# Two per-sample 64x64 channel mixes with residuals: the first loads reordered, the index column turned on TensorE

## The chip, the cores and the metric

One core of one Trainium2 chip runs the kernel. The metric is the device time of one execution in microseconds. The kernel before was timed three times: 92.57 us in the median, 92.44 to 92.94. All data is fp32, x and the output are 16.78 MB each.

## The reference

Both layers act on channels only, so one sample b needs one 64x64 matrix: with A = I + w0[subject[b]] and B = I + w1[condition[b]], the output is (A B) transposed, times x[b].

```python
def reference(x, itok_B_0_7, itok_B_1_198, L0_cond_weights, L1_cond_weights):
    # x (128, 64, 512); L0 weights (8, 64, 64); L1 weights (200, 64, 64)
    x = x + jnp.einsum('bct,bcd->bdt', x, L0_cond_weights[itok_B_0_7])
    x = x + jnp.einsum('bct,bcd->bdt', x, L1_cond_weights[itok_B_1_198])
    return x
```

## The kernel before

Everything of x fits in SBUF (`xy`, 128 KB of each partition) and is overwritten in place by the output, so loads never wait for a free buffer. The 128 samples are cut into 32 slots of four samples; two slots are a unit (8 samples, 1 MB of x), and there are 16 units.

**Start.** SyncE issues the condition indices `cond` (128 numbers, one to each partition, L129), then x of unit 0 (L130) and the first slot of unit 1 (L131). It then waits at L133 for `s_w0b_early`, which VectorE has finished raising when the 16 first-layer matrices of units 0 and 1 are picked, and issues the other slot of unit 1 and units 2 to 15 (L134 to L136). ScalarE issues the first-layer weights `w0_rows` (128 KB, L370) and the indices `subjects` (L372). GpSimd builds the identity matrix (L142, L144), waits for `cond` (L147) and issues the gather (L148): 128 rows of 16 KB of the second layer's weights, row b to partition b, 2.1 MB.

**First layer.** TensorE turns `w0_rows` (L171); VectorE adds the identity into `w0t` (L349) and copies the 16 picks of units 0 and 1 (L360). GpSimd copies the other 112 picks once the gather has landed (L163).

**Ticks.** From the landing of `w0_rows` ScalarE makes TICKS dummy copies (L378), and after each of them TensorE makes three dummy transposes (L176). They compute nothing that is used; TensorE meets its work behind them only when the last is done.

**Second layer.** When the gather has landed, VectorE adds 1 to the diagonals (L365), TensorE turns the matrices in 16 turns of four (L186), and VectorE and ScalarE copy them out of PSUM (L269) in turn. TensorE then multiplies the pairs of matrices (`products`, L206), VectorE and ScalarE write them to `m_diag` (L276, L295), and TensorE applies them to x (`apply_single` L247 for unit 0, `apply` L225 for the rest). Each result is copied over x by the two engines (L303, L282), and ScalarE issues one store for each finished unit (L312, L315), the last unit in two halves of 512 KB.

**Queues.** SyncE's DMAs are q1 in the profile, ScalarE's q10, GpSimd's gather q0. All of them run on the same 16 DMA engines.

Of the kernel before, what the change touches and what calls it, by code (L numbers as in the profile page):

```python
# [5 lines left out]
def bass_cond_residual_kernel(  # L6
# [24 lines left out]
    fp32 = mybir.dt.float32  # L31
    i32 = mybir.dt.int32
    ALU = mybir.AluOpType

    B, C, T = x_dram.shape
# [24 lines left out]
    EARLY = 2  # L60


    TICKS = 18
    WARM = 3
    POOL = mybir.EngineType.Pool
    DVE = mybir.EngineType.DVE
# [8 lines left out]
    with ctx:  # L75
        def sb(name, shape, dt):
            return ctx.enter_context(nc.sbuf_tensor(name, shape, dt))

        def sem(name):
            return ctx.enter_context(nc.semaphore(name))  # L80
# [7 lines left out]
        m_diag = sb("m_diag", [P, 2, M_RING, J, P], fp32)  # L88
        ident = sb("ident", [P, P], fp32)
        mask = sb("mask", [P, 2], fp32)  # L90
        cond = sb("cond", [B, 1], i32)
        subjects = sb("subjects", [1, B], i32)

        psum = ctx.enter_context(nc.psum_tensor("psum", [P, 8, BANK], fp32))
        w0_psum = psum[0:C, 7, :]

        s_cond = sem("s_cond")
        s_subjects = sem("s_subjects")
        s_w0_rows = sem("s_w0_rows")
# [19 lines left out]
        s_x = [sem(f"s_x{n}") for n in range(UNITS)]  # L119
# [4 lines left out]
        @block.sync  # L124
        def _(sp):
            def load(s, n):
                sp.dma_start(xy[:, s:s + n, :], x_view[:, s:s + n, :]).then_inc(s_x[s // 2], 16)

            sp.dma_start(cond[:, :], cond_dram.rearrange("(b o) -> b o", o=1)).then_inc(s_cond, 16)  # L129
            load(0, 2)  # L130
            load(2, 1)  # L131

            sp.wait_ge(s_w0b_early, EARLY * UNIT)  # L133
            load(3, 1)  # L134
            for v in range(2, UNITS):
                load(2 * v, 2)  # L136
            for v in range(UNITS):
                sp.wait_ge(s_out[v], 32 if v < SINGLE or v == UNITS - 1 else 16)

        @block.gpsimd  # L140
        def _(pool):
            nc.gpsimd.memset(ident[:, :], 0.0).then_inc(s_zeros, 1)  # L142
            pool.wait_ge(s_zeros, 1)
            nc.gpsimd.affine_select(out=ident[:, :], in_=ident[:, :], compare_op=ALU.not_equal, fill=1.0,  # L144
                                    base=0, pattern=[[-1, P]], channel_multiplier=1).then_inc(s_ident, 1)

            pool.wait_ge(s_cond, 16)  # L147
            nc.gpsimd.indirect_dma_start(  # L148
                out=w1_rows[:, :, :].rearrange("b d e -> b (d e)"), out_offset=None,
                in_=w1_dram.rearrange("s d e -> s (d e)"),  # L150
                in_offset=bass.IndirectOffsetOnAxis(ap=cond[:, 0:1], axis=0)).then_inc(s_gather, 16)

            pool.wait_ge(s_subjects, 16)
            for first in range(EARLY * UNIT, B, 2 * UNIT):
                _, picked = nc.values_load_multi_w_load_instructions(  # L155
                    subjects[0:1, first:first + 2 * UNIT], engines=(POOL,), min_val=0, max_val=S0 - 1,
                    skip_runtime_bounds_check_because="subjects index the 8 matrices")
                if first == EARLY * UNIT:
                    pool.wait_ge(s_gather, 16)
                    pool.wait_ge(s_w0t, 4)  # L160
                for n in range(2 * UNIT):
                    v, odd, r = (first + n) // UNIT, n // SLOT % 2, n % SLOT
                    nc.gpsimd.tensor_copy(w0b[HALVES[odd], v * SLOT + r, :],  # L163
                                          w0t[HALVES[odd], bass.ds(picked[n] * C, C)]).then_inc(s_w0b, 1)

        @block.tensor
        def _(pe):
            pe.wait_ge(s_ident, 1)
            pe.wait_ge(s_w0_rows, 16)
            for z in range(ROWS):  # L170
                last = nc.tensor.transpose(w0_psum[:, z * P:(z + 1) * P], w0_rows[:, z, :], ident[:, :])  # L171
# [39 lines left out]
            def apply(k):  # L211

                first, n = BLOCKS[k]
                pe.wait_ge(s_m_v, 2 * (k + 1))
                pe.wait_ge(s_m_s, 2 * (k + 1))
                for s in range(2 * first, 2 * (first + n)):
                    v, odd = s // 2, s % 2
                    pe.wait_ge(s_x[v], 32 if v == 1 else 16)
                    if s >= Y_RING:

                        pe.wait_ge(s_y_v, 2 * (s - Y_RING + 1))
                        pe.wait_ge(s_y_s, 2 * (s - Y_RING + 1))
                    for j in range(J):
                        for h, rows in enumerate(HALVES):
                            last = nc.tensor.matmul(psum[:, 2 * (s % Y_RING) + h, :],  # L225
                                                    m_diag[rows, odd, v % M_RING, j, :],
                                                    xy[rows, s, j * T:(j + 1) * T],
                                                    start=j == 0, stop=j == J - 1)
                    last.then_inc(s_y_psum, 1)

            def apply_single(k):

                v = BLOCKS[k][0]
                pe.wait_ge(s_m_v, 2 * (k + 1))
                pe.wait_ge(s_m_s, 2 * (k + 1))
                pe.wait_ge(s_x[v], 32 if v == 1 else 16)
                for half in range(2):
                    s = 2 * v + half
                    if s >= Y_RING:

                        pe.wait_ge(s_y_v, 2 * (s - Y_RING + 1))
                        pe.wait_ge(s_y_s, 2 * (s - Y_RING + 1))
                    for j in range(J):
                        for h in range(2):
                            rows = QUARTERS[2 * half + h]
                            for odd, columns in enumerate(HALVES):
                                last = nc.tensor.matmul(psum[columns, 2 * (s % Y_RING) + h, :],  # L247
                                                        m_diag[rows, odd, v, j, 0:C],
                                                        xy[rows, 2 * v + odd, j * T:(j + 1) * T],
                                                        start=j == 0, stop=j == J - 1)  # L250
                    last.then_inc(s_y_psum, 1)
# [83 lines left out]
        @block.vector  # L335
        def _(dve):
            for r, rows in enumerate(QUARTERS):
                for b in range(2):
                    nc.vector.memset(mask[rows, b:b + 1], 1.0 if b == r % 2 else 0.0).then_inc(s_mask, 1)

            dve.wait_ge(s_ident, 1)
            dve.wait_ge(s_subjects, 16)
            dve.wait_ge(s_w0_turned, 1)

            turned = w0_psum.rearrange("q (y j s k) -> q j s k y", y=J, j=J, s=S0)
            one = ident[0:C, 0:C].rearrange("q (o k y j) -> q j o k y", o=1, y=J, j=J)
            for rows in HALVES:
                for j in range(J):
                    nc.vector.tensor_tensor(  # L349
                        w0t[rows, :].rearrange("q (s j k y) -> q j s k y", s=S0, j=J, y=J)[:, j, :, :, :],  # L350
                        turned[:, j, :, :, :],
                        one[:, j, :, :, :].to_broadcast((C, S0, Q // J, J)), ALU.add).then_inc(s_w0t, 1)

            _, picked = nc.values_load_multi_w_load_instructions(
                subjects[0:1, 0:EARLY * UNIT], engines=(DVE,), min_val=0, max_val=S0 - 1,
                skip_runtime_bounds_check_because="subjects index the 8 matrices")
            dve.wait_ge(s_w0t, 4)
            for n in range(EARLY * UNIT):
                v, odd, r = n // UNIT, n // SLOT % 2, n % SLOT
                nc.vector.tensor_copy(w0b[HALVES[odd], v * SLOT + r, :],  # L360
                                      w0t[HALVES[odd], bass.ds(picked[n] * C, C)]).then_inc(s_w0b_early, 1)

            dve.wait_ge(s_gather, 16)
            diagonal = w1_rows[:, :, :].rearrange("b d e -> b (d e)")[:, ::C + 1]
            nc.vector.tensor_scalar_add(diagonal, diagonal, 1.0).then_inc(s_w1_plus, 1)  # L365
            copies(dve, nc.vector.tensor_copy, nc.vector.tensor_scalar_mul, s_w1_v, s_m_v, s_y_v, 0)

        @block.scalar
        def _(act):
            act.dma_start(w0_rows[:, :, :], w0_dram.rearrange("s (k j) d -> (s k) j d", j=ROWS)  # L370
                          ).then_inc(s_w0_rows, 16)
            act.dma_start(subjects[:, :], subject_dram.rearrange("(o b) -> o b", o=1)).then_inc(s_subjects, 16)  # L372

            act.wait_ge(s_w0_rows, 16)
            for n in range(TICKS):
                if n >= 1:
# [31 lines left out]
```

## Time and profile before

| | |
|---|---|
| median of three runs | 92.57 us |
| profiled execution | 92.7 us, of which the span is 90.8 us and 1.9 us lie around it |
| TensorE / VectorE / ScalarE / GpSimd busy | 85% / 66% / 63% / 26% of the span |
| moved by DMA | 35.93 MB, 396 GB/s over the span |
| mean granted TensorE clock | 0.968 |

Times inside the kernel count from the start of the span. "Share" of DMA is the busy share of the 16 DMA engines and can read slightly above 1. Bytes are booked in the slice in which a packet begins; a packet of the gather is 16 KB, one of x 4 KB, so short slices in the gather's time jump up and down.

### The profile page before, as it was taken

How to read it: one execution, taken by the hardware profiler on the slowest of the kernel's cores; microseconds unless marked ns; L12 is line 12 of the kernel's file. 1: busy time of each engine (PE TensorE's matmuls, PEld its weight loads, DVE VectorE, ACT ScalarE, POOL GpSimd, SP SyncE). 2: the span in 40 equal slices, each digit the busy share in tenths (PEclk: the TensorE clock that was granted, in tenths of full speed). 3: DMA queues.
4: the chain of work that ended last, by engine and by line, in shares of the span. 5: the costliest groups of instructions: out<-in, count | busy, mean ns of one | idle time of the engine just before them, and what ended most of it. 6: DMA issues, size and time to landing. Idle time of an engine off the chain costs nothing.

```text
span 90.8 us, 2458 instructions
## 1 busy us (share of the span) xinstructions
PE 76.8 (85%) x906; PEld 42.9 (47%) x906; DVE 60.0 (66%) x124; ACT 57.0 (63%) x114; POOL 23.5 (26%) x119
## 2 busy tenths in 40 slices
PE   0599959977999999999999999999999999992000
PEld 0489749965545443544544454454444444440000
DVE  1096019994388787978878788888787887887000
ACT  2899807885367675867776677777576775775000
POOL 3400049989998988000000000000000000000000
PEclk9999999999999999999999999999999999999755
DMA  0999999999999999999999999999999999999992
GB/s 6 337 446 424 455 361 415 420 399 409 409 413 402 409 418 394 419 418 424 411 415 426 415 413 420 420 422 420 411 415 422 420 419 428 404 424 420 419 399 103
DMA packets 9453, 35.93 MB, mean 396 GB/s; under 512 B 737, under 2 KB 866, under 8 KB 9314
## 3 DMA queue, kind: packets, MB, share of 16 engines
q1 hardware_dynamic: 4512, 16.78, 46.1%
q10 hardware_dynamic: 4786, 16.91, 45.8%
q0 software_dynamic: 144, 2.10, 5.4%
q8 instruction: 7, 0.11, 0.5%
q14 instruction: 4, 0.03, 0.1%
HBM read 19.01 MB, written 16.78 MB: 394 GB/s over the span
## 4 chain that ended last, share of the span: by engine, by line
PE 68%; DMA 12%; DVE 9%; issue 1%; DVEq 1%; ACTq 0%; POOLq 0%
PE psum L225 58%; DMA w_rows<-in_L_cond_weights_dram,cond 10%; DVE w L269 7%; PE psum L206 7%; PE psum L247 2%; DMA subjects<-in_itok_B_dram 2%; DVEq L75 1%; PE psum L186 1%; DVE xy L303 1%; ACTq L370 0%; DVE m_diag L276 0%; DVE w_rows L365 0%; POOLq L155 0%; DVEq L275 0%
## 5 line engine op out<-in xcount | busy, mean ns | idle before, releaser
L225 PE MATMUL psum<-xy,m_diag 64*128 64x512 f32 x240 | 53.4, 595 | 0.0
L303 DVE COPY xy<-psum 64x512 f32<-64x512 f32 x60 | 41.0, 684 | 11.1 <-PE psum L225 10.2
L303 ACT COPY xy<-psum 64x512 f32<-64x512 f32 x60 | 34.9, 582 | 17.5 <-PE psum L225 16.8
L225 PEld LDWEIGHTS psum<-xy,m_diag 64*128 64x128 f32 x240 | 22.6, 187 | 25.6 <-issue 25.0
L163 POOL COPY w0b<-w0t 64x64 f32 x112 | 21.7, 237 | 10.1 <-DMA w_rows<-in_L_cond_weights_dram,cond 8.2
L206 PEld LDWEIGHTS psum<-w,w0b 64*32 64x32 f32 x512 | 5.6, 105 | 6.4 <-issue 3.0
L269 ACT COPY w<-psum 64x256 f32<-64x256 f32 x16 | 5.8, 365 | 3.8 <-PE psum L186 2.8
L186 PE MATMUL psum<-ident,w_rows 128*64 128x128 f32 x64 | 7.2, 274 | 1.0 <-DVE w_rows L365 1.0
L378 ACT COPY w<-w_rows 128x256 f32<-128x256 f32 x18 | 7.3, 405 | 0.8 <-DMA w_rows<-in_L_cond_weights_dram 0.2
L186 PEld LDWEIGHTS psum<-ident,w_rows 128*64 128x64 f32 x64 | 7.0, 151 | 1.3 <-DVE w_rows L365 1.3
L206 PE MATMUL psum<-w,w0b 64*32 64x64 f32 x512 | 6.9, 224 | 0.9 <-DVE w L269 0.9
L269 DVE COPY w<-psum 64x256 f32<-64x256 f32 x16 | 6.7, 417 | 1.2 <-PE psum L186 0.8
L176 PE MATMUL psum<-ident,w_rows 128*64 128x128 f32 x54 | 7.5, 303 | 0.0
L176 PEld LDWEIGHTS psum<-ident,w_rows 128*64 128x64 f32 x54 | 6.5, 126 | 1.0 <-ACT w L378 0.4
L295 DVE TENSOR_SCALAR m_diag<-psum,mask 128x256 f32<-128x256 f32 (+1 forms) x16 | 6.7, 462 | 0.2
L295 ACT ACTIVATE m_diag<-psum,mask 128x256 f32<-128x256 f32 (+1 forms) x16 | 6.5, 460 | 0.2
L171 PE MATMUL psum<-ident,w_rows 128*64 128x128 f32 x4 | 1.0, 414 | 3.4 <-DMA w_rows<-in_L_cond_weights_dram 3.4
L349 DVE TENSOR_TENSOR w0t<-psum,ident 64x256 f32<-64x256 f32 x4 | 1.5, 412 | 3.3 <-PE psum L171 3.3
L365 DVE TENSOR_SCALAR w_rows<-w_rows 128x64 f32<-128x64 f32 x1 | 0.2, 225 | 4.0 <-DMA w_rows<-in_L_cond_weights_dram,cond 4.0
L282 DVE COPY xy<-psum 128x512 f32<-128x512 f32 x2 | 1.3, 686 | 1.8 <-PE psum L247 1.8
L378 ACT ACT_TABLE_LOAD x1 | 1.3, 1283 | 1.8 <-issue 1.8
L360 DVE COPY w0b<-w0t 64x64 f32 x16 | 2.1, 188 | 0.2
(14 smaller groups left out, 7.2 us busy)
## 6 DMA issues: line engine op xcount, KB each, us to landing
xy<-in_x_dram SPq DMA_DIRECT2D x15, 1024.0 KB, 19.7
out_dram<-xy ACTq DMA_DIRECT2D x14, 1024.0 KB, 14.4
out_dram<-xy ACTq DMA_DIRECT2D x4, 512.0 KB, 8.3
xy<-in_x_dram SPq DMA_DIRECT2D x2, 512.0 KB, 5.8
w_rows<-in_L_cond_weights_dram ACTq DMA_DIRECT2D x1, 128.0 KB, 2.5
cond<-in_itok_B_dram SPq DMA_DIRECT2D x1, 0.5 KB, 2.2
subjects<-in_itok_B_dram ACTq DMA_DIRECT2D x1, 0.5 KB
w_rows<-in_L_cond_weights_dram,cond POOLq DMA_INDIRECT x1, 9.2
```

Source lines behind the costliest of these rows:

```text
L163: nc.gpsimd.tensor_copy(w0b[HALVES[odd], v * SLOT + r, :], w0t[HALVES[odd], bass.ds(picked[n] * C, C)]).then_inc(s_w0b, 1)
L176: nc.tensor.transpose(psum[0:C, z, 0:P], w0_rows[:, z, :], ident[:, :])
L186: last = nc.tensor.transpose(psum[0:C, n % W1_RING, z * B:(z + 1) * B], w1_rows[:, :, n * TURN + z], ident[:, :])
L206: last = nc.tensor.matmul(psum[QUARTERS[r], M_BANKS[k] + odd, at:at + C], w0b[rows, v * SLOT + r, j * Q:(j + 1) * Q], w1[rows, v * SLOT + ...
L225: last = nc.tensor.matmul(psum[:, 2 * (s % Y_RING) + h, :], m_diag[rows, odd, v % M_RING, j, :], xy[rows, s, j * T:(j + 1) * T], start=j = ...
L247: last = nc.tensor.matmul(psum[columns, 2 * (s % Y_RING) + h, :], m_diag[rows, odd, v, j, 0:C], xy[rows, 2 * v + odd, j * T:(j + 1) * T], ...
L269: copy(w1[rows, :, n * TURN:(n + 1) * TURN].rearrange("q (v r) k -> q v r k", r=SLOT), turned[:, odd, :, :, :]).then_inc(done, 1)
L295: scale(to[:, b, :, :, :], psum[:, M_BANKS[k] + odd, at:at + n * J * C].rearrange("q (w e i) -> q w i e", i=J, e=Q), mask[:, b:b + 1]).the ...
L303: copy(xy[rows, s, i * T:(i + 1) * T], psum[HALVES[i], 2 * (s % Y_RING) + h, :]).then_inc(done, 1)
L349: nc.vector.tensor_tensor(w0t[rows, :].rearrange("q (s j k y) -> q j s k y", s=S0, j=J, y=J)[:, j, :, :, :], turned[:, j, :, :, :], one[:, ...
L360: nc.vector.tensor_copy(w0b[HALVES[odd], v * SLOT + r, :], w0t[HALVES[odd], bass.ds(picked[n] * C, C)]).then_inc(s_w0b_early, 1)
L378: nc.scalar.copy(w1[:, 0:ROWS, :], w0_rows[:, :, :]).then_inc(s_tick, 1)
```

## The change

ScalarE issues the condition indices as one run of 512 B into one partition (`cond_row`), ahead of `w0_rows`. VectorE copies them to fp32, TensorE turns them (a transpose of one row into one column of PSUM bank 6), VectorE copies the column to int32 `cond`, and GpSimd waits for that copy. SyncE issues x of unit 0 first, then the whole of unit 1, and only then waits for `s_w0b_early`. TICKS is 16. The semaphores and the two small tiles that this needs are added.

```diff
-    TICKS = 18
+    TICKS = 16
...
+        cond_psum = psum[:, 6, 0:1]
...
-            sp.dma_start(cond[:, :], cond_dram.rearrange("(b o) -> b o", o=1)).then_inc(s_cond, 16)
             load(0, 2)
-            load(2, 1)
+            load(2, 2)
 
             sp.wait_ge(s_w0b_early, EARLY * UNIT)
-            load(3, 1)
             for v in range(2, UNITS):
                 load(2 * v, 2)
...
-            pool.wait_ge(s_cond, 16)
+            pool.wait_ge(s_cond, 1)
...
             pe.wait_ge(s_ident, 1)
+            pe.wait_ge(s_cond_float, 1)
+            nc.tensor.transpose(cond_psum, cond_float[:, :], ident[0:1, 0:1]).then_inc(s_cond_turned, 1)
+
             pe.wait_ge(s_w0_rows, 16)
...
-                    pe.wait_ge(s_x[v], 32 if v == 1 else 16)
+                    pe.wait_ge(s_x[v], 16)
...
+            dve.wait_ge(s_cond_row, 16)
+            nc.vector.tensor_copy(cond_float[:, :], cond_row[:, :]).then_inc(s_cond_float, 1)
+            dve.wait_ge(s_cond_turned, 1)
+            nc.vector.tensor_copy(cond[:, :], cond_psum).then_inc(s_cond, 1)
+
             dve.wait_ge(s_ident, 1)
             dve.wait_ge(s_subjects, 16)
...
         def _(act):
+            act.dma_start(cond_row[:, :], cond_dram.rearrange("(o b) -> o b", o=1)).then_inc(s_cond_row, 16)
             act.dma_start(w0_rows[:, :, :], w0_dram.rearrange("s (k j) d -> (s k) j d", j=ROWS)
                           ).then_inc(s_w0_rows, 16)
```

## Rows read from the trace of the kernel before

**Rows 1.** The page, DMA packets.
```profile
DMA packets 9453, 35.93 MB, mean 396 GB/s; under 512 B 737, under 2 KB 866, under 8 KB 9314
```

**Rows 2.** Windows: stretch and length, busy by engine, PEclk, DMA share, GB/s.
```profile
6.00:12.00 6.00, 5.68 (x47) 4.80 (x45) 2.22 (x17) 4.76 (x12) 0.00 (x0) 1.00 1.01 426
20.00:80.00 60.00, 59.00 (x776) 28.19 (x778) 46.67 (x77) 40.92 (x77) 14.83 (x77) 1.00 1.03 415
89.00:89.50 0.50, 0.00 (x0) 0.00 (x0) 0.00 (x0) 0.00 (x0) 0.00 (x0) 0.50 0.52 213
```

**Rows 3.** Chain of waits, TensorE's last piece (start, length).
```profile
68.34 13.96 PE psum L225 x64
```

**Rows 4.** Timeline of the end: start us, us, engine line op.
```profile
83.75 0.35 ACTq L315 DMA_DIRECT2D out_dram<-xy  x1
```

**Rows 5.** Timeline of the start.
```profile
0.75 0.41 ACTq L370 DMA_DIRECT2D w_rows<-in_L_cond_weights_dram  x1
...
0.75 0.38 SPq L129 DMA_DIRECT2D cond<-in_itok_B_dram  x1
...
1.19 23.26 SPq L127 DMA_DIRECT2D xy<-in_x_dram  x13
1.20 0.54 ACTq L372 DMA_DIRECT2D subjects<-in_itok_B_dram  x1
...
3.26 1.12 POOL L148 DMA_INDIRECT w_rows<-in_L_cond_weights_dram,cond  x1 [1.76 <-DMA subjects<-in_itok_B_dram]
3.28 7.83 ACT L378 COPY w<-w_rows 128x256 f32<-128x256 f32 x18 [0.23 <-DMA w_rows<-in_L_cond_weights_dram]
...
6.24 2.22 DVE L360 COPY w0b<-w0t 64x64 f32 x16
...
12.44 0.23 DVE L365 TENSOR_SCALAR w_rows<-w_rows 128x64 f32<-128x64 f32 x1 [3.98 <-DMA w_rows<-in_L_cond_weights_dram,cond]
```

**Rows 6.** Timeline of SyncE, 3 to 9 us.
```profile
8.49 0.81 SPq L127 DMA_DIRECT2D xy<-in_x_dram  x2
```

**Rows 7.** DMA queues, 2 to 3 us: packets, MB, share of 16 engines.
```profile
q1 hardware_dynamic: 142, 0.07, 52.1%
q10 hardware_dynamic: 146, 0.13, 41.7%
```

**Rows 8.** DMA queues, 6 to 7 us (in 4 to 5 us only q1).
```profile
q1 hardware_dynamic: 94, 0.32, 79.3%
q0 software_dynamic: 15, 0.25, 57.4%
```

**Rows 9.** DMA queues, 11.5 to 12 us.
```profile
q1 hardware_dynamic: 32, 0.13, 69.2%
```

**Rows 10.** Timeline of the first store's issue.
```profile
26.67 0.75 ACTq L312 DMA_DIRECT2D out_dram<-xy  x1
```

**Rows 11.** DMA queues, 28 to 29 us.
```profile
q1 hardware_dynamic: 114, 0.42, 104.2%
```

**Rows 12.** DMA queues, 32 to 33 us.
```profile
q1 hardware_dynamic: 68, 0.27, 66.6%
q10 hardware_dynamic: 68, 0.14, 35.7%
```

**Rows 13.** The page, DMA issues: KB each, median us from issue to landing.
```profile
out_dram<-xy ACTq DMA_DIRECT2D x4, 512.0 KB, 8.3
w_rows<-in_L_cond_weights_dram ACTq DMA_DIRECT2D x1, 128.0 KB, 2.5
w_rows<-in_L_cond_weights_dram,cond POOLq DMA_INDIRECT x1, 9.2
```

**Rows 14.** The page, costliest groups (busy, mean ns of one, idle before).
```profile
L171 PE MATMUL psum<-ident,w_rows 128*64 128x128 f32 x4 | 1.0, 414 | 3.4 <-DMA w_rows<-in_L_cond_weights_dram 3.4
```

**Rows 15.** Waits of TensorE.
```profile
PE psum L186 <- DVE w_rows L365: 1.0, 1, 1.0
```

**Rows 16.** The first window of half a us with a lower clock.
```profile
85.00:85.50 0.50, 0.00 (x0) 0.00 (x0) 0.00 (x0) 0.00 (x0) 0.00 (x0) 0.55 0.99 410
```

More of the change, by code:

```diff
@@ L90, in bass_cond_residual_kernel @@
         mask = sb("mask", [P, 2], fp32)
+        cond_row = sb("cond_row", [1, B], i32)
+        cond_float = sb("cond_float", [1, B], fp32)
         cond = sb("cond", [B, 1], i32)
@@ L95, in bass_cond_residual_kernel @@
         w0_psum = psum[0:C, 7, :]
+        cond_psum = psum[:, 6, 0:1]
+        s_cond_row = sem("s_cond_row")
+        s_cond_float = sem("s_cond_float")
+        s_cond_turned = sem("s_cond_turned")
         s_cond = sem("s_cond")
@@ L235, in apply_single @@
                 pe.wait_ge(s_m_s, 2 * (k + 1))
-                pe.wait_ge(s_x[v], 32 if v == 1 else 16)
+                pe.wait_ge(s_x[v], 16)
                 for half in range(2):
```

## The prediction

> **What bounds the kernel now.** I read the page first. TensorE is busy 85% of the span and heads the chain of waits, so it looks like the bound. The end says otherwise: TensorE's last piece is over at 68.34 + 13.96 = 82.30 us [rows 3], the last store is issued at 83.75 [rows 4], and the span lasts to 90.8. The windows show what fills the rest: the DMA engines run at share 1.03 and 415 GB/s from 20 to 80 us, and are half busy at 89 [rows 2]. 35.93 MB [rows 1] at 415 GB/s are 86.6 us. DMA is the bound, from about 2.5 us to the end. How much TensorE may slip: the last store is out at 84.10; the 128 KB load took 2.5 us from issue to landing [rows 13], 512 KB need 0.39 MB more, 0.95 us; so it could be there at 87.5, where it lands near 89.7. TensorE has 2.2 us of slack, if the DMA queues never run dry.
>
> Then the start, where a hole could hide. The page's slices dip to 361 GB/s near 11 us, as if DMA starved between gather and x. But 16 KB packets are booked where they begin: the whole stretch 6 to 12 us has 426 GB/s and share 1.01 [rows 2]. The gather's first packets are in 6 to 7 us, x's last in the same slice [rows 8], and x is back at 11.5 to 12 [rows 9]. So x, gather and x follow each other without a hole, and **the only DMA time to be won lies before 3 us**: in 2 to 3 us just 0.20 MB were moved [rows 7], where 0.42 would fit.
>
> **The change part by part.**
>
> x first. SyncE issued the indices at 0.75 and x at 1.19 [rows 5]; x now goes at 0.75: 0.44 us earlier. But `w0_rows`, 0.13 MB, was moved in 2 to 3 us [rows 7], while x was not yet coming. It now travels inside the stream of x and costs 0.13 / 0.42 = 0.31 us of it. Sure gain: 0.44 - 0.31 = 0.13 us. From above: if x finds the descriptor path emptier than it did behind two other DMAs, it can also win half of the 0.22 MB that 2 to 3 us left unused, 0.26 us; with `w0_rows` still fitting in before x, up to 0.13 + 0.26 + 0.31 = 0.70. From below 0, if x's first data is bound by something else. I take 0.2, near the sure gain. The 128 small packets of `cond` lay in the same empty time: nothing.
>
> The index chain. The row of 512 B is like `subjects`: issued at 1.20, there about 2.0 us later, so `cond_row` at 2.75. Then a VectorE copy (the 64x64 one is 2.22 / 16 = 0.14 us with its gap), a transpose (at most 0.41 [rows 14]), another copy, and three signals: 0.6 to 0.8 us. The gather is issued at about 3.5, against 3.26 [rows 5]. TensorE and VectorE have nothing else then: `w0_rows` lands later still. This is hidden because the gather's data waits for x anyway: issued at 3.26, it began only about 6.7, as x's 1.57 MB ended [rows 8]. If the cover goes, it costs what the gather is late beyond x's end.
>
> 2 MB ahead. 0.52 MB more of x is 1.26 us at 415 GB/s. x and `w0_rows` end at 6.7 - 0.44 + 1.26 + 0.31 = 7.8. The gather (2.1 MB at 426, 4.9 us) ends at 12.8 where it ended at 11.6, and is seen 0.8 later (12.44 against 11.6): 13.6. Bytes ahead of the gather are bytes not behind it: nothing for DMA, but TensorE starts the second layer 1.2 us later. That is within its slack.
>
> SyncE's wait. L133 ended at 8.49 [rows 6], 5.24 us behind the landing of `w0_rows` at 3.25 (0.75 + 2.5 [rows 13]): TensorE's transposes, VectorE's four adds and 16 picks, ending at 6.24 + 2.22 = 8.46 [rows 5]. One issue less stands behind the wait, but all of units 2 to 15 does. x needs some 1.3 us from issue to first bytes (issued at 1.19, moving in 2 to 3 [rows 7]), so SyncE must be free by 11.5, and `w0_rows` must land by 6.2. ScalarE issues it at 1.20 in place of 0.75, now behind `cond_row` and beside x. When does it land? Sharing with x at once: near 4.2. Behind x's first unit (1.05 MB, 2.5 us): near 5.7. Both fit; no hole.
>
> **Weighed against the skill.** The trace shows how a newcomer is served [rows 10 to 12]: a store issued at 26.67 has moved nothing in 28 to 29, where x has the engines alone, and at 32 to 33 both queues have 68 packets each. So a DMA first waits for what is already taken in (over 2 us), then takes turns. The Trainium skill (DMA: Bandwidth & Descriptors, Queues, rings and completion order) says that each engine goes round between queues with work, a whole packet of some 9 to 17 descriptors at a time. By that rule `w0_rows` would wait for one DMA of x at most and land at 5.7 or before: no hole, 92.4. By the rows, turns come after the backlog and piece by piece, which is the first rival. The rows of 32 to 33 us fit either reading of "turns"; the wait of 28 to 29 us is shown by the rows alone.
>
> Ticks. 18 took 7.83 us, 0.435 each [rows 5]; 16 take 6.96. TensorE's last tick was done 8.4 us behind `w0_rows` (12.72 - 1.04 [rows 15] - 3.25), now 7.6: at 11.8 to 13.3 by the two landings, before the second layer's 13.9. The idle gap is 0.6 to 2.1 us where it was 1.0. The granted clock was full for the 2.2 us after TensorE's end at 82.30 and fell only in 85.0 to 85.5 [rows 16], to its lower level of 1.2 GHz. So a gap of 2.1 should keep 2.4 GHz. Nothing.
>
> **Sum.** 92.7 (profiled execution, 90.8 of span and 1.9 around it) - 0.2 = 92.5. That execution lies 0.13 above the median of the runs: 92.4.
>
> **The rivals.**
>
> 1. *SyncE is released too late; DMA runs dry behind the gather* (slower side). `w0_rows` waits for the first unit of x and then takes turns with unit 1: each 1 KB of it behind 4 KB of x, 0.13 x 5 / 0.42 = 1.6 us, so it lands at 2.5 + 2.5 + 1.6 + 0.35 = 6.9. SyncE goes on at 12.2, x moves at 13.5, the gather ended at 12.8: a hole of 0.7, 93.1. Behind both units of x it lands at 8.2, the hole is 2.0 and TensorE's start slips 3.1 us: 94.4. It decides from a landing of 6.2 on. For it: the first store's wait [rows 10, 11]. Against: unit 1 of x is issued no earlier than `w0_rows`, and `subjects`, issued together with x before, was not held up by it.
> 2. *The indices come late.* `cond_row` is issued together with x and waits for the first unit: 5.2 in place of 2.75. The gather is issued at 5.9. It took 3.4 us from issue to first data before, part of that waiting; so 7.0 to 9.3 against x's end at 7.8. Hole 0 to 1.5, in the middle 0.4: 92.8, at worst 93.9. For: the tie at 0.75. Against: one packet on one engine, and a quicker issue.
> 3. *The head of DMA gains more*: x flows 0.5 to 0.7 us sooner in effect, 91.9 to 92.1.
> 4. *TensorE's clock falls* in a longer gap and the second layer's 8 us run slower by some: the slack takes up to 1.0 us of it (2.2 - 1.2). This decides only together with rival 1.
>
> **Chances.** Measurement tells about 0.5% (0.46 us) from no change. Forecast, no hole and a small gain, 0.44. Rival 3, 0.24. Rival 1 with the hole near 0.7, 0.18 (0.08 of it inside 0.46 us); with 2.0, 0.06. Rival 2, 0.08, counted as slower. So faster 0.24, same 0.52, slower 0.24. The range 92.0 to 93.4 takes in the gain's bounds but for its last tenth and the smaller hole; outside are 0.08 below and 0.11 above.
>
> **What would show it.** SyncE's first issue of x at 0.75. Landing of `w0_rows` between 4 and 6 us. First packets of the gather at 7.5 to 8 us, with x ending in that slice, and x back at 12.5 to 13 with no window under 400 GB/s over 12 to 20 us. `m_diag` about 1.2 us later, TensorE's end near 83.5. A SyncE that goes on after 11.5 us makes the forecast wrong, and so does a gather that starts with x long done.

## The result, and the profile after

The changed kernel takes 94.24 us in the median of six runs, the kernel before, run beside it, 92.70: a ratio of 1.0163, 95% interval 1.0124 to 1.0202. It is slower by 1.6%, where no change was forecast (92.4, range to 93.4). The profiled execution took 94.08 us with a span of 92.3. Rival 1 of the prediction is what happened: SyncE was let go too late. The time is near that of its dearer form (94.4); the part on the prediction shows that the mechanism is that of the cheaper one.

Timeline of the start of the changed kernel (start us, us, engine line op), which answers to [rows 5]:

```profile
0.75 0.54 ACTq L383 DMA_DIRECT2D cond_row<-in_itok_B_dram  x1
...
0.75 25.36 SPq L133 DMA_DIRECT2D xy<-in_x_dram  x12
...
1.32 0.37 ACTq L384 DMA_DIRECT2D w_rows<-in_L_cond_weights_dram  x1
...
2.02 0.21 DVE L350 CAST cond_float<-cond_row 1x128 f32<-1x128 int32 x1 [0.72 <-DMA cond_row<-in_itok_B_dram]
...
2.65 0.16 DVE L352 CAST cond<-psum 128x1 int32<-128x1 f32 x1 [0.42 <-PE psum L175]
3.10 1.12 POOL L152 DMA_INDIRECT w_rows<-in_L_cond_weights_dram,cond  x1 [1.61 <-DVE cond L352]
7.69 6.96 ACT L392 COPY w<-w_rows 128x256 f32<-128x256 f32 x16 [4.29 <-DMA w_rows<-in_L_cond_weights_dram]
...
10.60 2.22 DVE L373 COPY w0b<-w0t 64x64 f32 x16
13.54 0.23 DVE L378 TENSOR_SCALAR w_rows<-w_rows 128x64 f32<-128x64 f32 x1 [0.72 <-DMA w_rows<-in_L_cond_weights_dram,cond]
```

The index chain is quick: the gather is issued at 3.10, earlier than the 3.26 of before. The first-layer weights are what went wrong. Issued at 1.32, they are used from 7.69 on, where before that was 3.28. VectorE's early picks end at 10.60 + 2.22 = 12.82, and SyncE goes on right behind them. Timeline of SyncE in the changed kernel, 12 to 13 us, against the 8.49 of [rows 6]:

```profile
12.84 0.37 SPq L133 DMA_DIRECT2D xy<-in_x_dram  x1
```

The windows of the changed kernel show what that costs (stretch and length; busy time of TensorE, its weight loads, VectorE, ScalarE and GpSimd; PEclk, the granted TensorE clock as a share of full speed; DMA share; GB/s):

```profile
0.00:20.00 20.00, 12.52 (x95) 11.74 (x96) 8.11 (x40) 10.68 (x25) 7.71 (x38) 1.00 0.86 330
12.00:13.00 1.00, 1.00 (x10) 1.00 (x9) 0.78 (x7) 0.91 (x4) 0.00 (x0) 1.00 0.62 262
13.00:14.00 1.00, 1.00 (x12) 1.00 (x11) 0.23 (x1) 0.94 (x3) 0.30 (x2) 1.00 0.58 45
14.00:15.00 1.00, 1.00 (x12) 1.00 (x10) 0.00 (x0) 0.62 (x2) 0.94 (x6) 1.00 0.36 139
15.00:16.00 1.00, 1.00 (x12) 1.00 (x10) 0.00 (x0) 0.00 (x0) 0.94 (x6) 1.00 1.03 414
20.00:80.00 60.00, 58.94 (x787) 29.87 (x787) 46.80 (x80) 40.87 (x80) 15.66 (x82) 1.00 1.03 414
```

The same first 20 us of the kernel before:

```profile
0.00:20.00 20.00, 15.51 (x122) 14.00 (x122) 10.28 (x44) 13.71 (x34) 8.66 (x43) 1.00 0.91 361
```

By 20 us the kernel before has moved 361 x 20 = 7.22 MB, the changed one 330 x 20 = 6.60. From there on both run at 414 to 415 GB/s. The missing 0.62 MB are 1.5 us at that rate, as much as the loss (94.24 - 92.70 = 1.54). But for two, which move next to nothing, the gather's last packets begin in 12 to 13 us. Of x, 11 packets begin in 13.75 to 14, the next in 14.5 to 14.75, and only from 14.75 on is it near its full rate (393 GB/s): the queue ran dry.

### The profile page after: what moved, and what is told of

Same layout as the page of the kernel before. It is cut to its first block, busy times and chain, and to the rows that moved or that the text cites. A ratio compares the mean times of both kernels' runs of the same rounds, so it can differ in the third digit from the quotient of the medians.

```text
span 92.3 us, 2447 instructions
## 1 busy us (share of the span) xinstructions
PE 76.5 (83%) x901; PEld 43.5 (47%) x901; DVE 60.4 (65%) x126; ACT 56.2 (61%) x112; POOL 23.4 (25%) x119
## 4 chain that ended last, share of the span: by engine, by line
PE 75%; DVE 8%; DMA 7%; issue 1%; DVEq 1%; ACTq 1%
PE psum L233 57%; PE psum L184 7%; DVE w L277 7%; DMA w_rows<-in_L_cond_weights_dram 7%; PE psum L214 7%; PE psum L255 2%; PE psum L179 1%; DVEq L75 1%; DVE xy L311 1%; ACTq L383 1%; PE psum L194 0%; DVE m_diag L284 0%; DVEq L283 0%
## 5 line engine op out<-in xcount | busy, mean ns | idle before, releaser
L233 PEld LDWEIGHTS psum<-xy,m_diag 64*128 64x128 f32 x240 | 23.1, 187 | 25.2 <-issue 24.6
L392 ACT COPY w<-w_rows 128x256 f32<-128x256 f32 x16 | 6.5, 405 | 4.8 <-DMA w_rows<-in_L_cond_weights_dram 4.3
```

The lines of the kernel that those rows point to most:

```text
L233: last = nc.tensor.matmul(psum[:, 2 * (s % Y_RING) + h, :], m_diag[rows, odd, v % M_RING, j, :], xy[rows, s, j * T:(j + 1) * T], start=j = ...
L392: nc.scalar.copy(w1[:, 0:ROWS, :], w0_rows[:, :, :]).then_inc(s_tick, 1)
```

## The experiments

Two theories stood against each other. **Dry queue**: SyncE is let go too late, DMA idles behind the gather, and nothing gives the time back. **TensorE late**: its second layer starts at 15.5 in place of 12.7, and that is more than its slack. Ratios are to the kernel before, run beside each.

### Let SyncE go earlier, in the changed kernel

```diff
-            sp.wait_ge(s_w0b_early, EARLY * UNIT)
+            sp.wait_ge(s_w0t, 1)
```

> The changed kernel with SyncE waiting for the first of VectorE's four adds into w0t instead of the last of its 16 early picks. In the changed kernel the picks ended near 12.8 us and the gather's last packets began before 13. Theory 'dry queue' (DMA has nothing to do for about 1.8 us because SyncE is let go too late): SyncE goes on at 9.3 to 9.5, x follows the gather without a hole, and the time falls by 1.5 to 2 us to 92.2 to 92.7 although TensorE starts the second layer as late as before (15.4). Rival 'TensorE late' (its chain slipped 2.7 us, more than its slack): no more than 0.3 us are won, 93.9 to 94.3.

Measured: 92.71 us, ratio 0.9975 (0.9957 to 0.9994), as the dry queue has it. Its windows:

```profile
0.00:20.00 20.00, 12.32 (x97) 11.33 (x98) 8.35 (x41) 10.87 (x26) 7.67 (x38) 1.00 0.93 364
13.00:14.00 1.00, 1.00 (x12) 0.95 (x9) 0.24 (x2) 0.91 (x3) 0.26 (x2) 1.00 1.04 422
80.00:86.00 6.00, 4.80 (x24) 1.85 (x20) 4.92 (x8) 4.32 (x8) 0.00 (x0) 1.00 0.97 391
```

One wait moved from 12.84 to 9.56 takes back the whole loss, though TensorE starts the second layer at 15.25, nearly as late as in the change. Its first 20 us move 364 GB/s, 0.06 MB more than the kernel before, worth 0.14 us, and the sure gain of the prediction's sum was 0.13. This is one execution of each, though: the four profiled kernels with x first and no hole moved 361 to 364 GB/s in their first 20 us, the five with x at 1.19 and no hole (the kernel before among them) 359 to 362. The last row shows something new: DMA is no longer quite full before the end (391 GB/s, where the kernel before has 419). That is TensorE's lateness, small once the hole is gone.

### Let SyncE go later, in the kernel before

```diff
-            sp.wait_ge(s_w0b_early, EARLY * UNIT)
+            sp.wait_ge(s_gather, 16)
```

> The kernel before with SyncE waiting for the gather to land (12.4 us) instead of the early picks (8.49), nothing else. Theory 'dry queue': DMA idles from 11.6 until about 1.9 us behind the next issue, 14.3; a hole of 2.7 us that nothing gives back: 95.2 to 95.6, although TensorE's chain does not move (second layer at 12.7). Rival 'TensorE late': the chain has not moved, so 92.7 to 93.2.

Measured: 95.49 us, ratio 1.0285 (1.0246 to 1.0323), as the dry queue has it, with TensorE's second layer at 13.15. Its windows:

```profile
0.00:20.00 20.00, 15.84 (x121) 14.73 (x122) 9.88 (x43) 13.40 (x33) 8.25 (x41) 1.00 0.80 304
12.00:15.00 3.00, 2.36 (x22) 2.09 (x21) 1.31 (x4) 0.69 (x2) 1.86 (x10) 1.00 0.36 98
```

(361 - 304) x 20 = 1.14 MB are missing at 20 us, 2.7 us at 415 GB/s. The time rose by 2.6. A hole in this queue costs its length.

### TensorE's chain alone: fewer ticks in the changed kernel, more in the one before

```diff
-    TICKS = 16
+    TICKS = 12
```

> The changed kernel with 12 ticks in place of 16; nothing else. ScalarE's dummy copies end 1.74 us sooner, so TensorE starts the second layer at about 13.8 in place of 15.4. Theory 'dry queue': the DMA hole stays, the time stays at 94.2 within 0.3. Rival 'TensorE late': 1.2 to 1.6 us are won, 92.6 to 93.0.

Measured: 94.0 us, ratio 1.0115 (1.0062 to 1.0169). TensorE started 1.7 us sooner (13.79) and almost nothing came back. What did come back the bytes account for: in this profile the weights came at 7.04 and SyncE went on at 12.19, 0.65 sooner, and the first 20 us moved 340 GB/s in place of 330, 0.5 us worth. Against the kernel before (361) that is 0.42 MB or 1.0 us too little, and this execution took 93.72 us, 1.0 more than the profiled one of before.

In the kernel before, TICKS = 27 in place of 18:

> The kernel before with 27 ticks in place of 18 and nothing else: TensorE's second layer starts near 15.6 in place of 12.7, a slip of 2.8 us, about that of the changed kernel (2.7), while SyncE, the loads and the gather are untouched. It prices the late TensorE chain alone. Theory 'dry queue' with a slack of about 2.5 to 3: the last store is issued near 86.6, 0 to 0.4 us are lost, ratio 1.000 to 1.004. If TensorE's lateness were what slowed the changed kernel, the ratio would be its 1.016.

Measured: 92.93 us, ratio 1.0017 (0.9997 to 1.0036). The second layer starts at 15.45, as in the changed kernel (15.52), and the time hardly moves. One line of its timeline and one of its windows:

```profile
15.45 7.15 PE L186 MATMUL psum<-ident,w_rows 128*64 128x128 f32 x64
```

```profile
80.00:86.00 6.00, 5.06 (x24) 2.23 (x20) 4.92 (x8) 4.31 (x8) 0.00 (x0) 1.00 0.96 391
```

TensorE's lateness is worth at most 0.4% (the interval's upper end), not 1.6. Theory "TensorE late" falls.

### 2 MB of x ahead of the gather, alone

The kernel before, with this edit and the one that it needs (TensorE's two waits for unit 1 count one load in place of two):

```diff
             load(0, 2)
-            load(2, 1)
+            load(2, 2)
 
             sp.wait_ge(s_w0b_early, EARLY * UNIT)
-            load(3, 1)
```

> The kernel before with the whole of unit 1 (0.5 MB more of x) issued ahead of SyncE's wait, nothing else: indices, first-layer weights and 18 ticks as before. Theory 'dry queue': the order of bytes changes, not their sum, the first-layer weights land at 3.25 as before, SyncE goes on at 8.5 while the gather now ends at 12.8; the same time within 0.3 us of 92.7, the gather 1.2 us later. Rival 'TensorE late' would give 0 to 0.5 more for a chain that starts 1.2 us later.

Measured: 93.71 us, ratio 1.0103 (1.0055 to 1.0152), which neither theory expected. Its six runs spread from 93.12 to 94.85 us, and the profiled execution is the fastest of them. Its windows and its waits of TensorE:

```profile
14.00:15.00 1.00, 0.02 (x1) 0.02 (x1) 0.23 (x1) 0.00 (x0) 0.14 (x1) 0.68 1.06 434
15.00:16.00 1.00, 1.00 (x5) 0.88 (x6) 0.00 (x0) 0.00 (x0) 0.94 (x6) 0.50 0.99 401
80.00:86.00 6.00, 5.85 (x28) 2.32 (x24) 4.64 (x8) 3.81 (x8) 0.00 (x0) 1.00 0.86 346
```

```profile
PE psum L185 <- DVE w_rows L364: 3.1, 1, 3.1
```

There is no hole at the start, since SyncE went on at 8.53, and the first 20 us move 362 GB/s. But the gather is seen at 14.7 in place of 12.4, while TensorE's 18 ticks end at 11.9. TensorE idles 3.1 us, its granted clock falls to 1.2 GHz, and the second layer starts late and slow. The last store is issued at 87.33 and DMA lacks work before it (346 GB/s).

The extra 0.52 MB of x explain 1.26 us of the gather's delay of 2.26. The other 1.0 us nobody had expected, and its cause is open. It comes again with 23 ticks (14.71) and when SyncE issues the weights (14.91, below), but not in the early-release kernel (13.59). In the first three SyncE goes on at 8.1 to 8.6, in the last at 9.56. With 23 ticks in the same kernel:

> The kernel before with 2 MB of x ahead of the gather and 23 ticks in place of 18. With 18 ticks TensorE idled 3.06 us ahead of the second layer, its granted clock fell to 0.5 until past 16 us, the last store was issued at 87.33, and the time rose by 1%. Theory 'clock': 23 ticks end near 14.1, the clock stays full, the second layer starts at 14.7 to 14.9 at 2.4 GHz and the time is that of the kernel before plus 0 to 0.3: 92.8 to 93.2. Rival 'bytes' (0.5 MB more of x ahead of the gather costs by itself, by a later chain or by turns with the gather): still 93.5 to 93.8.

Measured: 92.91 us, ratio 1.0006 (0.9991 to 1.0021). The wait is 1.0 us, the clock stays full, the 64 turns start at 14.99 as before them (14.98) and take 7.2 us in place of 8.5. So the order of the bytes is free, and the clock was the price. The changed kernel didn't pay it because its ticks began 4.4 us late: they ended at 15.5, after the gather was seen (13.54).

### The order of the first issues

In the changed kernel, ScalarE issues `w0_rows` ahead of `cond_row`, with 22 ticks:

> The changed kernel with ScalarE issuing the first-layer weights ahead of the index row, and 22 ticks, SyncE's wait as in the change. Theory 'who is taken in first': the weights, issued at 0.75 together with x, land near 3.3 to 4 in place of 7.65, or wait for x's first 16 packets per DMA engine and land near 5.3; SyncE goes on at 8.5 to 10.6 and no hole follows the gather. The index row, issued at 1.2, is behind x's first unit and lands near 5.4; the gather is issued near 6.4 and its data comes at 8 to 9.5, with a hole of 0.5 to 1.5 between x (done near 8) and the gather: 93.2 to 94.2. If the weights land later than 7, the theory on the order is wrong.

Measured: 94.57 us, ratio 1.0165 (1.0141 to 1.019). The weights, issued in the same instant as x, are used from 5.26 on: even in a tie they come 2 us later than alone ahead of x (3.28, [rows 5]), and 2.4 us sooner than issued at 1.32. In 3 to 4 us the two queues have 79 and 78 packets: here the turns begin with unit 0. The index row, now second, is used only at 6.01, and the gather is issued at 7.09. A hole follows between x and the gather: 78 GB/s for 8 to 9 us. It is rival 2 of the prediction. SyncE goes on at 11.66, later than the 8.5 to 10.6 expected, since TensorE turned the weights only behind the indices (6.53); behind the gather DMA is at share 0.80 in 14 to 15 us. The time lies 0.4 us above the expected 93.2 to 94.2. The first 20 us of the profiled execution, 95.47 us and so 0.9 above the median, moved 314 GB/s, 2.3 us less than the kernel before.

Next, SyncE issues `w0_rows` itself, ahead of x, and ScalarE `cond_row`, again with 22 ticks:

> The changed kernel with SyncE issuing the first-layer weights ahead of x (x then goes at about 1.2, as in the kernel before), the index row alone ahead of subjects on ScalarE, 22 ticks, SyncE's wait as in the change. Theory 'dry queue': the weights land at 3.2, SyncE goes on at 8.5, no hole; x starts as in the kernel before, so nothing is won at the start: ratio 0.998 to 1.003. If x's head start were worth nothing in the early-release kernel either, this one would equal it; the theory says it is 0.2 to 0.4 slower than 12 ticks with early release.

Measured: 93.59 us, ratio 1.0061 (1.0037 to 1.0084). That is above the expected 0.998 to 1.003. The weights come at 2.97 and SyncE goes on at 8.12, as expected or sooner, and the first 20 us move 359 GB/s, so there is no hole to speak of. But the gather is seen at 14.9, TensorE's ticks end at 13.1, and this happens (timeline, then windows):

```profile
15.19 8.88 PE L196 MATMUL psum<-ident,w_rows 128*64 128x128 f32 x64 [2.07 <-DVE w_rows L380]
```

```profile
15.00:16.00 1.00, 0.81 (x7) 0.81 (x8) 0.24 (x2) 0.00 (x0) 0.88 (x5) 1.00 1.03 418
16.00:17.00 1.00, 1.00 (x7) 0.85 (x6) 0.73 (x2) 0.49 (x2) 0.94 (x6) 0.50 1.01 406
```

A gap of 2.07 us was enough: the clock fell to 1.2 GHz at 16, 0.8 us after it, with TensorE busy again. The last store is issued at 87.89, and the span ends 3.9 us later at 91.8, as it did in the run with 2 MB alone (87.33 and 91.3). In all the others 4.2 to 9.1 us lie between the two. So about 3.9 us are the least that the span lasts beyond the last store's issue. In the kernel before that gives 83.75 + 3.9 = 87.7 against a span of 90.8: an estimated slack of 3.1 us, not the 2.2 of the prediction. It does not end sharply: in the kernels without a hole and with last stores at 86.2 to 86.5, DMA is already below its full rate in 80 to 86 us (391 to 404 GB/s).

### Can the changed kernel be made to win?

Early release and 12 ticks together:

> The changed kernel with both edits: SyncE let go by the first add into w0t, and 12 ticks. With the early release alone the hole was gone, the last store was issued at 86.28 and DMA fell to share 0.97 and 391 GB/s in 80 to 86 us. Theory 'two bounds' (once the hole is gone, TensorE's late chain, 15.25 where the gather was seen at 13.6, starves the stores at the end): the second layer starts near 13.8, the last store is issued near 84.9, DMA is full to 88, and x's earlier start is worth 0.3 to 0.4 at last: 92.2 to 92.5, ratio 0.992 to 0.996 to the kernel before. Rival 'DMA alone' (the chain has slack in the early release too): no change from it, ratio 0.997 to 0.998.

Measured: 92.72 us, ratio 0.9999 (0.9981 to 1.0018). In its profile TensorE started the second layer at 15.12, hardly sooner than with the early release alone (15.25). Two things stood against it. The index row came 0.85 us later than in the others, and with it the gather (seen at 14.37):

```profile
2.87 0.21 DVE L350 CAST cond_float<-cond_row 1x128 f32<-1x128 int32 x1 [1.57 <-DMA cond_row<-in_itok_B_dram]
```

In the other six profiled kernels that issue the row first, this cast begins at 2.02 or 2.03. Yet TensorE didn't wait for the gather: it was still at its dummy transposes, which is the second thing. Those of the changed kernel and of this one (ns: shortest, median, longest; then first and last start):

```profile
L184 PE MATMUL psum<-ident,w_rows x48: 272/273/421, 8.6 to 15.4; 128*64 128x128 f32 x48
L184 PE MATMUL psum<-ident,w_rows x36: 272/417/418, 8.7 to 15.0; 128*64 128x128 f32 x36
```

In every kernel they start slowly, at 6 or 7 in a microsecond, and later run at up to 12; here the slow stretch lasted to nearly 14 us, in the kernel before to under 7. The granted clock reads 1.00 all along, so it doesn't show this. ScalarE was done with its 12 copies at 13.08, but TensorE's transposes behind them were not. So the expectation wasn't tested; why the row came late once, and why the slow stretch was long, is open.

Then 1.5 MB of x ahead as before, SyncE let go when TensorE has turned the weights, and 12 ticks; and the same with unit 1 held back until the index row is there, and 14 ticks:

```diff
             load(0, 2)
-            load(2, 2)
+            sp.wait_ge(s_cond_row, 16)
+            load(2, 1)
...
-            sp.wait_ge(s_w0b_early, EARLY * UNIT)
+            sp.wait_ge(s_w0_turned, 1)
+            load(3, 1)
```

(The first of the two has no wait on `s_cond_row`.)

> The changed kernel with the 1.5 MB of x ahead of the gather that the kernel before had, SyncE let go as soon as TensorE has turned the first-layer weights (about 8.4), and 12 ticks. In the runs so far either DMA had a hole (changed kernel), or TensorE's chain started at 15 and the last store, issued at 86.3 to 86.9, set the end 3.2 to 3.7 us later (early release with 16 and 12 ticks). Theory 'two bounds': no hole, second layer at 12.9 to 13.4, last store near 84.2 to 84.6 with DMA at share above 1 to 88, and x's earlier start (first MB through at 5.05 in place of 5.45) shows in full: ratio 0.994 to 0.997 to the kernel before. Rival 'no gain to be had' (what x gains at the start is paid back by the weights inside its stream): 0.998 to 1.002.

> The same with SyncE waiting for the index row to land before it issues the first half of unit 1, and 14 ticks: the first-layer weights then have only x's first unit ahead of them, not turns with unit 1. Theory 'taken in first': they land at 5.6 to 6.0 in place of 7 to 7.9, TensorE's turning ends by 7, the rest as in the run beside it; time equal to it within 0.3, 92.3 to 92.6. If the weights still land near 7, it is not the turns with unit 1 that held them.

Measured: 92.72 us, ratio 0.999 (0.9968 to 1.0013), and 92.77 us, ratio 1.0003 (0.9975 to 1.0031). Both are level with the kernel before, and the rival "no gain to be had" stands. The first is a weak test of it, since its second layer started at 14.14 and its last store was issued at 86.18, where 84.2 to 84.6 was expected. The second is a fair one: second layer at 13.53, last store at 84.89, DMA at share 1.02 in 80 to 86 us, and no gain. It also settles why the weights were late. From its timeline, then its DMA queues in 5 to 5.5 us:

```profile
6.13 6.08 ACT L394 COPY w<-w_rows 128x256 f32<-128x256 f32 x14 [2.79 <-DMA w_rows<-in_L_cond_weights_dram]
```

```profile
q10 hardware_dynamic: 125, 0.12, 66.5%
q1 hardware_dynamic: 32, 0.08, 39.2%
```

With only x's first unit ahead of them they come at 6.13, where in the run beside it, with half of unit 1 issued at 1.23, it is 7.54: turns with unit 1 cost about 1.4 us, the wait behind unit 0 the rest. (In the five profiled kernels with these turns the weights are used from 7.04 to 7.89 on, so the size is rough.) Here the half unit is issued at 2.02, 0.7 us behind the weights, and it doesn't take turns with them: 125 of their 128 packets go in half a microsecond, beside 32 of x.

## Why the prediction was wrong

**The step that failed is the landing of `w0_rows`.** The prediction put it at 4.2 to 5.7 and held that it must come by 6.2; it came at about 7.65 (issued at 1.32, 6.3 us to landing). The store's wait behind a filled queue [rows 10, 11] had shown it, and rival 1 had worked out 6.9, but the forecast set that reading aside. The DMA queues of the changed kernel, 4 to 5 and then 6 to 7 us, show it as rival 1 had it:

```profile
q1 hardware_dynamic: 103, 0.42, 102.6%
...
q1 hardware_dynamic: 81, 0.33, 80.5%
q10 hardware_dynamic: 80, 0.08, 22.8%
```

First the weights have nothing, while x's unit 0 is served; then both queues have the same number of packets, 81 and 80, of 4 KB and 1 KB. "Unit 1 is issued no earlier than the weights", held against the rival, was wrong: SyncE's second issue came at 1.23, before theirs at 1.32.

The mechanism is the cheaper form of rival 1, turns with unit 1, and not the dearer one, a wait behind both units. The turns began at 5.25 and took 1.75 us, against 5.0 and 1.6 in the rival, and from the last of their data at 7.0 to the landing it was 0.65 us, against 0.35. That the time came out near the dearer form's 94.4 is chance: to the cheaper form's 93.1 come the 0.75 us by which the weights were later than its 6.9, and 0.4 for the restart below, together 94.25.

**The Trainium skill's rule**, weighed in the prediction (DMA: Bandwidth & Descriptors, Queues, rings and completion order), gave a landing of 5.7 or before and 92.4 us. Neither holds. Once past the backlog, the turns in these rows go packet by packet, not in runs of 9 to 17: in each quarter of a microsecond from 5.5 to 7 the weights have 18 to 24 packets and x has 18 to 23. The 128 packets took 13.8% + 22.8% of the 16 engines' time in two windows of 1 us, 0.37 us, and yet 1.75 us to pass.

**The restart was priced too low.** I took 1.3 us from issue to first bytes. SyncE issued at 12.84, and the first packets did begin by 14; but they were 11, and the next came after 14.5. 13 to 15 us moved 0.045 + 0.139 = 0.18 MB, 0.44 us worth. Counted in bytes x was back at 14.56, 1.7 us behind the issue. SyncE was 1.34 late against the limit of 11.5, the restart 0.4 longer, the gain 0.14: 1.6 together, against 1.54 measured.

**The gain at the start** was taken as 0.2 and is 0.14 by the early-release run's first 20 us, 0.2 by its time (interval 0.06 to 0.43%), and nothing by the times of the three kernels after it. No run shows more, so the bound from above, 0.7, and with it rival 3 had too much of the chance.

**Right**: that DMA bounds the kernel from its first bytes, that the dip near 11 us was no hole, that the index chain is hidden (the gather is issued at 3.10, and its data comes in 7 to 8 us, where x ends), and that bytes ahead of the gather cost DMA nothing.

**Slack and clock**: the slack is about 3.1 us, not 2.2, so TensorE's 2.8 us (12.72 to 15.52) did not matter in the change, which the run with 27 ticks shows. The 89.7 that the 2.2 rests on stands in no row. "A gap of 2.1 should keep 2.4 GHz" is wrong, as the run with a gap of 2.07 shows, though [rows 16] have the clock full even to 85.0, 2.7 us behind TensorE's end.

The loss is settled by its removal, and by making it in the kernel before. What the change could have brought is about the 0.25% of the early-release run (interval 0.06 to 0.43%), and three neighbours of it gave none.

## What to carry to other kernels

Where DMA is the bound, add up the bytes moved by the time the kernel is in its steady state: divided by the steady rate, their deficit was the loss in the changed kernel, with 16 ticks and with 12, and in the kernel before with a hole made on purpose. It says nothing of what is lost at the end, as the run with 2 MB ahead shows: full at the start, slower all the same. Issue a small load that gates the next issue ahead of the large ones, also ahead of those on other queues: here it stood behind the megabyte issued before it and took turns with what was issued at nearly the same time. A wait that throttles a queue should hang on the earliest event that serves, with some 2 us to spare for the restart. Dummy work that keeps the clock up has to be timed again whenever its start or the thing that it waits for moves.

## What the runs showed of the hardware

- 128 KB took 6.3 us from issue to landing behind x on another queue, where they took 2.5 with nothing ahead. They waited for all of x's unit 0, issued 0.57 us before them, then alternated packet by packet with unit 1, issued 0.09 us before them. With half of unit 1 issued 0.7 us behind them instead, they passed in half a microsecond.
- From an issue on idle queues to nearly the full rate of x took 1.9 us (12.84 to 14.75), 1.7 us when counted in bytes.
- The granted clock fell after a gap of only 2.07 us, and when TensorE was busy again. The 64 turns took 8.9 us in place of 7.15. A gap of 1.03 us left it full.
- The first dummy transposes behind TensorE's idle start took about 420 ns each and later ones 272, with the granted clock at 1.00 throughout; the slow stretch ended between 5 and 14 us, differently from kernel to kernel.
- The 128 indices landed as one run of 512 B at about 2.0 us and were on their partitions, through VectorE, TensorE and VectorE again, at 2.81. As 128 packets they let the gather go at 3.26; so this part of the change does win 0.16 us, off the critical path.
